# Attention scores: one f32 product or three bf16 products of high and low parts

## The reference, cut to what matters

```
q = l2norm(xn @ w_q) * q_scale          # per head, 64 wide
k = l2norm(xn @ w_kv[:, :1024]) * k_scale   # two learned null keys go ahead of the 1024
sim = 8 * q @ k.T - slope_h * |j - i - 2|   # causal: keys past the query are masked
out = softmax(sim) @ v;   x = layernorm(x + out @ w_out)
```

## Time and profile before

| | us |
|---|---|
| median of 3 runs | 1975.85 (1969.0 to 1978.14) |
| the profiled execution | 1974.28 |
| its span, first to last instruction | 1972.5 |
| mean granted TensorE clock, of full | 0.916 |
| PE busy | 1632.6 |
| DVE busy | 1096.6 |
| ACT busy | 760.9 |
| POOL busy | 562.7 |

### The profile page before, as it was taken

How to read it: one execution, slowest core, us unless ns; L and a number is a source line. 1 busy time by engine, 2 the same in 40 slices (tenths; PEclk the granted TensorE clock), 3 DMA queues, 4 the chain that set the end, 5 groups by cost and what they waited for, 6 DMA issues and landing times. The chain is left out here.

```text
span 1972.5 us, 28814 instructions
## 1 busy us (share of the span) xinstructions
PE 1632.6 (83%) x8973; PEld 766.2 (39%) x8974; DVE 1096.6 (56%) x2591; ACT 760.9 (39%) x1253; POOL 562.7 (29%) x557
## 2 busy tenths in 40 slices
PE   2699999999999999999999999844973777776777
PEld 1244444444444444443444444443651332232332
DVE  4246556546556655655655655562225666667664
ACT  2345444454454454454454454302431322322221
POOL 1342442442532533533533533152002011110000
PEclk9799999999999999999999999956995887887788
DMA  5501021020220220220220200041110000000000
GB/s 169 159 1 59 16 73 49 25 73 12 62 73 4 70 73 1 73 73 1 73 73 1 73 4 1 1 156 43 47 41 12 6 11 11 11 11 6 0 6 11
DMA packets 109361, 82.02 MB, mean 42 GB/s; under 512 B 5601, under 2 KB 101113, under 8 KB 108974
## 3 DMA queue, kind: packets, MB, share of 16 engines
q1 hardware_dynamic: 107182, 76.15, 12.6%
q0 software_dynamic: 2048, 4.20, 0.7%
HBM read 31.57 MB, written 48.76 MB: 41 GB/s over the span
## 5 line engine op out<-in xcount | busy, mean ns | idle before, releaser
L689 ACT ACTIVATE P<-S,keyb 128x386 f32<-128x386 f32 (+7 forms) x512 | 296.3, 629 | 414.3 <-PE S L490 403.4
L486 PE MATMUL S<-QT,KT 64*128 64x512 f32 (+5 forms) x1792 | 373.1, 473 | 12.7 <-DVE KT L816 11.0
L992 POOL TENSOR_TENSOR rn<-nm,half 128x12 f32<-128x12 f32 x128 | 323.8, 2539 | 23.6 <-DVE nm L753 23.6
L851 DVE TENSOR_TENSOR Psum<-Psum,P 128x1796 f32<-128x1796 f32 (+7 forms) x256 | 287.8, 1124 | 36.2 <-PE O L510 18.4
L1008 POOL TENSOR_SCALAR_AFFINE_SELECT P<-P 128x256 f32<-128x256 f32 (+1 forms) x256 | 117.2, 458 | 620.4 <-ACT P L689 620.3
L510 PE MATMUL O<-P,V 128*64 128x512 f32 (+5 forms) x1536 | 256.7, 437 | 13.9 <-POOL P L1008 11.8
L486 PEld LDWEIGHTS S<-QT,KT 64*128 64x128 f32 (+1 forms) x1792 | 156.5, 178 | 202.9 <-issue 194.0
L162 POOL TENSOR_TENSOR norm_rstd<-norm_vareps,half 128x4 f32<-128x4 f32 x40 | 40.9, 1023 | 481.5 <-DVE norm_vareps L147 481.4
L381 PE MATMUL W<-xT,wts 128*128 128x512 f32 x256 | 142.8, 653 | 15.0 <-DVE QT L812 7.2
L490 PE MATMUL S<-GQ,GK 64*128 64x512 bf16 (+5 forms) x896 | 148.7, 301 | 0.0
L873 DVE TENSOR_TENSOR part<-W,rden 128x512 f32<-128x512 f32 x128 | 82.2, 683 | 91.0 <-PE W L558 91.0
(11 more groups left out here) (214 smaller groups left out, 2221.2 us busy)
## 6 DMA issues: line engine op xcount, KB each, us to landing
xg<-zero SPq DMA_DIRECT2D x16, 1216.0 KB, 8.9
yg<-zero SPq DMA_DIRECT2D x16, 1216.0 KB, 11.9
xT<-xnt SPq DMA_DIRECT2D x16, 512.0 KB, 4.6
wts<-in_w_qkv SPq DMA_DIRECT2D x16, 384.0 KB, 5.6
gu<-in_gu SPq DMA_DIRECT2D x1, 2816.0 KB, 10.3
xb<-xg SPq DMA_DIRECT2D x40, 64.0 KB, 1.8
yg<-yb SPq DMA_DIRECT2D x40, 64.0 KB, 1.6
X<-in_x SPq DMA_DIRECT2D x8, 256.0 KB, 4.5
```

Of the source, the lines that this page charges most:

```text
L486: nc.tensor.matmul(S[hh][0:m, at + c:at + c + w], KT[d, r, p, jt * P:jt * P + m], QT[d, r, p, Q0[jt] + c:Q0[jt] + c + w], start=True, stop ...
L689: nc.scalar.activation(probs(p, jt)[0:m, hh, 0:n], S[hh][0:m, at:at + n], ACT.Exp, bias=keyb[0:m, r, (2 * p + hh) * NKT + jt:(2 * p + hh) ...
L851: nc.vector.tensor_tensor(x, x, probs(p, jt)[0:m, :, 0:NQ[jt]], ALU.add).then_inc(add_ok, 1)
L992: nc.gpsimd.tensor_tensor(rn[:, c, u], nm[:, c, u], powers, ALU.pow).then_inc(rn_ok, 1)
```

## The change

The score product is written as three bf16 products. q and k each have a high part (rounded to bf16) and a low part (what is left, rounded to bf16); high times high, high k times low q, and low k times high q are summed in PSUM, and low times low is left out. `QT` and `KT` get a leading index of part and become bf16. DVE's `scale` now writes a float32 buffer `full` with one slot for q and one for k; ACT's new `high` copies it to the bf16 high part; DVE's new `low` subtracts that from `full` into the low part. `scale` number i of a turn waits for `low` number i - 2, `low` waits for its `high`, and the scores of pair p wait for six (p = 0) or eight (p = 1) lows of their turn. The null keys get high and low parts once at the start on POOL. In `AT`, E1, R1, S10 and S11 stand half a step to a step earlier.

```diff
-                  "R0": "11a", "S00": "12b", "S01": "12b", "S02": "13b", "S03": "13b", "E1": "14b",
-                  "R1": "15a", "S10": "16a", "S11": "16b", "S12": "18a", "S13": "18a"}
+                  "R0": "11a", "S00": "12b", "S01": "12b", "S02": "13b", "S03": "13b", "E1": "14a",
+                  "R1": "14b", "S10": "15a", "S11": "15b", "S12": "18a", "S13": "18a"}
...
                     if jt == 0:
-                        for k in SPREAD[1][2 * p:2 * p + 2]:
-                            pe.wait_ge(prep_ev[BANK[k]], emptied(t, k))
+                        pe.wait_ge(low_ok, 8 * t + 4 + 2 * p + 2)
...
-                            nc.tensor.matmul(S[hh][0:m, at + c:at + c + w], KT[d, r, p, jt * P:jt * P + m],
-                                             QT[d, r, p, Q0[jt] + c:Q0[jt] + c + w], start=True, stop=False)
+                            nc.tensor.matmul(S[hh][0:m, at + c:at + c + w], KT[d, 0, r, p, jt * P:jt * P + m],
+                                             QT[d, 0, r, p, Q0[jt] + c:Q0[jt] + c + w], start=True, stop=False)
+                        for kpart, qpart in ((0, 1), (1, 0)):
+                            for hh in range(2):
+                                d = slice(hh * DH, (hh + 1) * DH)
+                                nc.tensor.matmul(S[hh][0:m, at + c:at + c + w], KT[d, kpart, r, p, jt * P:jt * P + m],
+                                                 QT[d, qpart, r, p, Q0[jt] + c:Q0[jt] + c + w], start=False, stop=False)
...
+                def high(n, r, c, j):                       # ACT
+                    k = SPREAD[c][j]
+                    act.wait_ge(prep_ev[BANK[k]], emptied(n, k))
+                    hold(act)
...
+                    nc.scalar.copy(dst, full[:, j % 2, :]).then_inc(high_ok, 1)
...
                             if AT[PROJ[c][j]][:-1] == str(s):
                                 evict(n, c, j)
                                 square(n, c, j)
+                            if AT[SPREAD[c][j]][:-1] == str(s):
+                                high(n, r, c, j)
...
                         if s == 0 and (not isinstance(t, int) or t):
                             pair_out(t - 1, 1)
+                            prepare(t, r, 18)
...
+                    i = 8 * n + 4 * c + j                   # DVE, scale
+                    if not isinstance(i, int) or i >= 2:
+                        dve.wait_ge(low_ok, i - 1)
...
-                        nc.vector.scalar_tensor_tensor(QT[:, r, j // 2, 512 * c:512 * c + 512], raw[:, c, j, :], scl[:, 2:3], W[BANK[k]][:],
+                        nc.vector.scalar_tensor_tensor(full[:, 0, :], raw[:, c, j, :], scl[:, 2:3], W[BANK[k]][:],
...
+                def low(n, r, c, j):
+                    dve.wait_ge(high_ok, 8 * n + 4 * c + j + 1)
+                    nc.vector.tensor_tensor(piece(1, r, c, j), full[:, j % 2, :], piece(0, r, c, j), ALU.subtract).then_inc(low_ok, 1)
...
                     if at == "12b":
                         parts(n, 1)
+                    for c, j, place in ((0, 0, "12b"), (0, 1, "12b"), (0, 2, "13b"), (0, 3, "13b"), (1, 0, "15b"), (1, 1, "16a"),
+                                        (1, 2, "18a"), (1, 3, "18a")):
+                        if place == at:
+                            low(n, r, c, j)
```

More of the change, by code:

```diff
@@ L188, in build @@
             nkT = sb("nkT", [P, 2 * NG, NNULL], F32, sc)
+            nkp = sb("nkp", [P, 2, 2 * NG, NNULL], BF16, sc)
             scl = sb("scl", [P, 3], F32, sc)
@@ L215, in build @@
             GQ = sb("GQ", [P, 2, 2, SEQ], BF16, sc)
-            QT = sb("QT", [P, 2, 2, SEQ], F32, sc)
-            KT = sb("KT", [P, 2, 2, NKEY], F32, sc)
+            full = sb("full", [P, 2, 512], F32, sc)
+            QT = sb("QT", [P, 2, 2, 2, SEQ], BF16, sc)
+            KT = sb("KT", [P, 2, 2, 2, NKEY], BF16, sc)
             V = sb("V", [P, 2, NKT, KW], F32, sc)
@@ L243, in build @@
             summed, x_sum = s1("summed"), s1("x_sum")
+            full_ok, high_ok, low_ok, nkh_ok, nkl_ok = s1("full_ok"), s1("high_ok"), s1("low_ok"), s1("nkh_ok"), s1("nkl_ok")
             STEPS = 2 * NKT
@@ L659, in edges_out @@
                                    W[BANK[k]][:].bitcast(BF16).rearrange("p (a n) -> p a n", a=2)).then_inc(prep_ev[BANK[k]], 1)
+                def high(n, r, c, j):
+                    k = SPREAD[c][j]
+                    act.wait_ge(prep_ev[BANK[k]], emptied(n, k))
+                    hold(act)
+                    if j % 2 == 0:
+                        dst = QT[:, 0, r, j // 2, 512 * c:512 * c + 512]
+                    else:
+                        dst = KT[:, 0, r, j // 2, NNULL + 512 * c:NNULL + 512 * c + 512]
+                    nc.scalar.copy(dst, full[:, j % 2, :]).then_inc(high_ok, 1)
                 def prepare(n, r, s):
@@ L722, in _ @@
                     nc.scalar.copy(nkT[hh * DH:(hh + 1) * DH], src[hh * DH:(hh + 1) * DH, :, hh, :]).then_inc(null_te, 1)
-                for s in range(STEPS):
+                for s in range(STEPS + 1):
                     prepare(0, 0, s)
@@ L809, in scale, with piece @@
                     dve.wait_ge(prep_ev[BANK[PROJ[c][j]]], emptied(n, PROJ[c][j]))
+                    i = 8 * n + 4 * c + j
+                    if not isinstance(i, int) or i >= 2:
+                        dve.wait_ge(low_ok, i - 1)
                     hold(dve)
                     if j % 2 == 0:
-                        nc.vector.scalar_tensor_tensor(QT[:, r, j // 2, 512 * c:512 * c + 512], raw[:, c, j, :], scl[:, 2:3], W[BANK[k]][:],
+                        nc.vector.scalar_tensor_tensor(full[:, 0, :], raw[:, c, j, :], scl[:, 2:3], W[BANK[k]][:],
                                                        ALU.mult, ALU.mult).then_inc(prep_ev[BANK[k]], 1)
                     else:
-                        at = NNULL + 512 * c
-                        nc.vector.tensor_tensor(KT[:, r, j // 2, at:at + 512], raw[:, c, j, :], W[BANK[k]][:],
-                                                ALU.mult).then_inc(prep_ev[BANK[k]], 1)
+                        nc.vector.tensor_tensor(full[:, 1, :], raw[:, c, j, :], W[BANK[k]][:], ALU.mult).then_inc(prep_ev[BANK[k]], 1)
+                def piece(part_, r, c, j):
+                    if j % 2 == 0:
+                        return QT[:, part_, r, j // 2, 512 * c:512 * c + 512]
+                    return KT[:, part_, r, j // 2, NNULL + 512 * c:NNULL + 512 * c + 512]
+                def low(n, r, c, j):
+                    dve.wait_ge(high_ok, 8 * n + 4 * c + j + 1)
+                    nc.vector.tensor_tensor(piece(1, r, c, j), full[:, j % 2, :], piece(0, r, c, j), ALU.subtract).then_inc(low_ok, 1)
                 def prepare(n, r, at):
@@ L981, in tables @@
                     nc.gpsimd.tensor_copy(keyb[:, r], tabs[:, bass.ds(n % NG, 1), 0:HG * NKT].rearrange("p a n -> p (a n)")).then_inc(tab_ok, 1)
-                    nc.gpsimd.tensor_copy(KT[:, r, :, 0:NNULL], nkT[:, bass.ds((n % NG) * 2, 2), :]).then_inc(nk_ok, 1)
+                    nc.gpsimd.tensor_copy(KT[:, :, r, :, 0:NNULL], nkp[:, :, bass.ds((n % NG) * 2, 2), :]).then_inc(nk_ok, 1)
                 def root(n, c, u):
@@ L1029, in _ @@
                 nc.gpsimd.tensor_copy(keyb[:, 0], tabs[:, 0, 0:HG * NKT]).then_inc(tab_ok, 1)
-                nc.gpsimd.tensor_copy(KT[:, 0, :, 0:NNULL], nkT[:, 0:2, :]).then_inc(nk_ok, 1)
+                nc.gpsimd.tensor_copy(nkp[:, 0], nkT[:]).then_inc(nkh_ok, 1)
+                pool.wait_ge(nkh_ok, 1)
+                nc.gpsimd.tensor_tensor(nkp[:, 1], nkT[:], nkp[:, 0], ALU.subtract).then_inc(nkl_ok, 1)
+                pool.wait_ge(nkl_ok, 1)
+                nc.gpsimd.tensor_copy(KT[:, :, 0, :, 0:NNULL], nkp[:, :, 0:2, :]).then_inc(nk_ok, 1)
                 for s in range(STEPS):
```

## The result

The changed kernel takes 2015.12 us (median of 4 runs, 2010.21 to 2018.89) where the one before takes 1973.01 (4 runs, 1969.0 to 1978.14): ratio 1.0188, interval 1.0155 to 1.022, some 42 us slower. The forecast had +14 to the median of before known then.

What follows compares the result with a forecast made beforehand. PE was taken to bound steps 0 to 8 of a turn, DVE its tail. 1974.3 + 15 (fifteen turns) - 4 (last turn) + 4 (turn 0) = 1989.3, forecast 1990 us at the runs' median; range 1944 to 2040.

Steps and rivals of the forecast that it cites:

- The body, -3.2 a turn: A turn outside its tail, bound by PE: three bf16 passes for four float32 ones save 3.2 us a turn.
- B: Rival, faster: only S02's wait grows, by 1.24 us, roots' copy in time at S10; 1946 us, chance 0.20 with neighbours.
- The tail, +4.2: From the values at 673.38 to the next turn's scores: six lows and six highs lengthen it by 4.2 us.
- exponentials behind high 5: Tail, step 16: ACT makes the exponentials after high 5, at 692.5 to 693.1; POOL cuts to 693.6, values end at 694.05.
- Places: nothing: Moving edges and roots one place up gains nothing; S10 moved up can't come earlier, as DVE's copy sets it.
- POOL's powers bound steps 11 and 12: Savings there count for nothing: POOL's three powers take 8.41 us; PE's wait for step 11's cut grows 0.6 to 1.3.
- The turn, +1.0: A whole turn: body -3.2 plus tail +4.2 gives +1.0 us, bounds -0.7 to +2.2.
- rival A: PE's longer idle gaps in the tail lower its clock: +4 us a turn, 2050, or 2010 in a third; chance 0.20.
- C: Rival, cheap ends: lows near 0.43 us, highs hidden, tail +3.0, a turn -0.2 to 0.2; 1973 to 1979, chance 0.11.
- D: Rival: the three products are no shorter than the float32 one, so the body saves nothing; 2041 us, chance 0.05.

Runs made afterwards that it cites:

- the run without parts: Changed kernel with scaling writing the bf16 high part itself, no highs or lows (low parts zero), old places: 1928.67 us, 0.9755 to the kernel before.
- the reordered one: Changed kernel with DVE's lows 0 and 1 behind the output scaling, 2 and 3 behind the roots' copy, `add`s of steps 14 and 15 late: 2015.94 us, 1.0207.

## Why the prediction was right in its direction and short in its size

**The body, -3.2 a turn: right at full clock.** The products took 0.66 for a predicted 0.70, and with the clock held up the body is 3.15 us shorter. In the changed kernel 1.6 of it arrives on average, and 0.8 in the turn shown. Two slips stand in its sum. Its own terms, 2.4 and 0.9 less 0.1 to 0.5 and less 0.1, make 2.7 to 3.1 and not 3.2; and chunks of 130 and 2 columns hold 5.7% of the columns, since steps of 642 and 514 end in them too, and not 2.9%. By the same terms B's lower end, no growth of the tail, is 1928 and not 1915. None of this moves the forecast out of its range.

**The tail, +4.2: right.** Measured +4.5 at full clock, +4.9 with the fall. Its terms: lows 0.69 (start to start 0.60; used 0.62, though the second of the pair shown, beside POOL's cut, took 0.90), highs 0.62, the roots' copy +2.6 later (+2.7), the wait ahead of S02 3.01, and 3.4 at most (3.4 said), the wait at S10 1.99 at full clock (2.3). In the changed kernel that last wait is hardly there (0.7 in 11 turns): PE at half clock comes to S10 later than the copy. A wait that is missing from the table was paid in slow matmuls. The last values' wait for POOL, 1.81 in the turn shown and 2.6 to 2.8 in others (the table's 36.8 us hold it and the wait at step 11), is partly my "exponentials behind high 5", and partly cuts of 0.94 to 1.24 us for 0.4 (the row at 630.26 holds one of 0.94 and a small one of 2 partitions), which I had not priced.

**Places: nothing. Wrong.** The sentence was "edges and roots one place up are the same MMs ... the move gains nothing there". Gains nothing is right; costs nothing was not looked at. In the float32 kernel the tail grew by 0.7 us at full clock (S10's wait 0.56, and POOL's cut uncovered in front of the last values), by 1.6 where the clock falls for some 3 us and by 3 where it falls for some 7, and this with no bf16 part in it. In the changed kernel the parts' delays cover that cost.

**POOL's powers bound steps 11 and 12: right.** The wait behind them was to grow from 0.6 to 1.3 and is 1.0. PE's busy time fell by 25 us and not by 60; the rest is matmuls that ran at half clock.

**The turn, +1.0: +1.35 at full clock.** The sum, 1989, is also what the changed kernel takes once idle products hold the clock (1988.67), but partly by luck. Set the three profiled executions against each other. From the start to S00's scaling in turn 0 (146.35 before) I had +0.8; it is -3.5 (142.88): the first scores come 1 us later (89.07 for 88.05) and not 4, and turn 0 saves 4.5 in its body. From the last turn's preparation on I had 0; it is +4.9 (776.4 for 771.5): the last turn saves 1.2 up to its last scores and not 4. It runs 10 us of that at half clock; in the run without parts, which has no fall there, it saves 4.8. The 14 turns between make +43.1 for a forecast of 14: 78.4 us a turn for 75.3. With idle products in the gaps they make +16.9. The two ends cancel; the turns' 26 do not.

**The failed step is rival A's dismissal.** It says of the falls, "1.89 us in the tail before did not", and gave them 0.20, so the sum of a turn has nothing for the clock. The clock made 26 of the 42 us, 1.9 us a turn (78.4 against 76.5), for a priced 4 in every turn or in a third of them. Of the parts of that 4, the loss in the next turn's scores was right (1.6 priced, 1.5 measured in the body); in the tail, where 2.5 were priced, it was 0.4, as slow matmuls there run in part in time in which PE would have waited. The dismissal rested on one turn, 614.70 to 689.80. Elsewhere in the same trace the same wait had gone with a fall; PE rows and windows of the kernel before:

```profile
377.63 0.38 PE L444 MATMUL W<-RT,selr 24*128 24x512 bf16 x1 [1.90 <-DVE part L873]
```

```profile
378.00:380.00 2.00, 1.79 (x14) 0.81 (x15) 2.00 (x4) 0.20 (x1) 0.00 (x0) 1.00 0.00 0
380.00:382.00 2.00, 2.00 (x12) 0.77 (x8) 1.91 (x2) 0.85 (x2) 0.41 (x1) 0.53 0.00 0
```

It fell at 380 and at 455, in two turns of sixteen, and these two took 76.6 and 76.7 us for 75.1. Windows over all turns would have shown that the kernel before already paid this now and then with its one gap, and a change that lengthens that gap and adds a second was likely to pay it more often; 0.20 was too little. The other argument against A, that PE works 3.9 us between the gaps, fell too: the clock was already at 0.50 in that work. The Trainium skill ("TensorE: Matmul & The Clock Gate", HAM oscillation), named there, says that idle gaps between bursts put the array back to its slower clock; the trace agrees (0.50 behind the gaps, gone when they are filled).

**Rivals.** B falls: the copy was not in time and the body's gain was not larger than the tail's loss. C falls: lows take 0.60 from start to start, not 0.43; with lows of two columns the turn is 75.0, within C's -0.2 to 0.2 of before, so its ground was real. D falls by the run without the parts.

**Shown and open.** Shown, by filling gaps and changing nothing else: the clock's 26 us in the changed kernel, 49 in the reordered one, and 16 or more of the places alone. Open is what decides whether one gap is followed by a fall: 1.89 mostly was not, 1.75, 1.66 and 1.04 were. These are the last or longest waits ahead of a fall and seldom the only ones: ahead of the 1.04, S02 had waited 1.90 and S10 0.56 in the same 10 us. The work around the gaps differs too, and no run varies that by itself. That POOL's cuts are slow because DVE works beside them was seen, not tried. What the idle products cost by themselves in the changed kernel was not separated; elsewhere it was 0 to 0.3 us a turn.

## What to carry to other kernels

When an edit shortens one engine's work and hands parts to the engine that ends a stage, replay the stage, and then ask what the first engine's new idle time does to its clock: read the granted clock over all turns, not one, and take a fall that already occurs in a few as a sign that longer gaps will make it the rule. Where a gap can't be closed, a few idle products in it that depend on nothing late tell at once what the clock costs, and can be left in: 13 a turn were worth 49 us here, which brought the reordered kernel level with the one before, not clearly past it. An edit of places that keeps the instructions still has to be priced for the cover that it takes from others.

## What the runs showed of the hardware that was not expected

- Idle products on PE cost the kernel before nothing (0.997, the same 75.07 us a turn) and took 49 us, 2.4%, off the reordered one, though they make PE execute more.
- POOL's cut of 256 columns took 0.40 to 0.41 us wherever no DVE instruction ran beside it (67 cuts of the kernel before). Beside DVE's `add`s and lows it took up to 1.24 in the tail of the changed kernel and 1.76 in that of the reordered one, and up to 1.33 in the kernel before, in the middle of a turn; beside the output scaling, which reads PSUM, it stayed at 0.41 (47 cuts). A row of the kernel before:

```profile
644.14 1.32 POOL L1008 TENSOR_SCALAR_AFFINE_SELECT P<-P 128x256 f32<-128x256 f32 x1 [4.22 <-ACT P L689]
```

- A low (float32 less bf16, written as bf16) took 0.69 us for 512 columns, no less than the same operation all in float32; ACT's cast of 512 took 0.62.
